# Turning gathered rows with a transposing DMA instead of TensorE, from the fourth tile of a mixture-of-experts layer on

## The reference, cut to what matters

```python
xt = x.reshape(b * l, d)
S = jax.nn.sigmoid(xt @ Wg)
G, I = jax.lax.top_k(S, TOP_K)
h = jax.nn.gelu(jnp.einsum('nd,edf->enf', xt, W1) + b1[:, None, :])
y = jnp.einsum('enf,efd->end', h, W2) + b2[:, None, :]
combine = jnp.zeros((N, E), dtype=x.dtype).at[jnp.arange(N)[:, None], I].add(G)
out = jnp.einsum('ne,end->nd', combine, y)
```

## Time and profile before

| | |
|---|---|
| median of three runs | 334.2 us (334.05 to 336.1) |
| the profiled execution | 335.84 us |
| its span, first to last instruction | 333.9 us |
| TensorE busy | 302.5 us (91%) |
| VectorE, ScalarE, GpSimd busy | 250.0, 179.7, 161.7 us |
| mean granted TensorE clock | 0.964 of full speed |
| DMA traffic | 39.41 MB, 118 GB/s over the span |

### The profile page before, as it was taken

How to read it: one execution, slowest core, us unless ns; L and a number is a source line. 1 busy time by engine, 2 the same in 40 slices (tenths; PEclk the granted TensorE clock), 3 DMA queues, 4 the chain that set the end, 5 groups by cost and what they waited for, 6 DMA issues and landing times.

```text
span 333.9 us, 8685 instructions
## 1 busy us (share of the span) xinstructions
PE 302.5 (91%) x3050; PEld 228.3 (68%) x3050; DVE 250.0 (75%) x596; ACT 179.7 (54%) x507; POOL 161.7 (48%) x162
## 2 busy tenths in 40 slices
PE   8999999999411898999999999999999999999991
PEld 8777534566311486888888888878777888877760
DVE  5898796779899799888888888887764656566441
ACT  4557484626815285676666667666534444434430
POOL 2415902556410732664456573365566647646353
PEclk9999999999955899999999999999999999999997
DMA  7400000011578294878667877764344544344421
GB/s 238 159 2 1 2 0 1 0 64 63 184 237 253 69 302 149 206 200 204 194 197 180 219 174 223 167 181 78 69 69 84 82 89 73 66 76 64 64 26 12
DMA packets 36361, 39.41 MB, mean 118 GB/s; under 512 B 8448, under 2 KB 32992, under 8 KB 36320
## 3 DMA queue, kind: packets, MB, share of 16 engines
q1 hardware_dynamic: 29344, 29.56, 30.1%
q0 software_dynamic: 6976, 9.31, 16.2%
HBM read 29.74 MB, written 9.11 MB: 116 GB/s over the span
## 4 chain that ended last, share of the span: by engine, by line
PE 58%; DMA 18%; DVE 13%; issue 6%; POOL 3%; POOLq 2%; ACT 0%
DMA out<-xt,idx 17%; PE ps L918 10%; PE ps L762 6%; PE ps L903 5%; PE ps L905 5%; PE ps L907 5%; PE ps L919 5%; PE ps L743 4%; PE ps L771 2%; PE ps L775 2%; PE ps L778 2%; PE ps L694 2%; PE ps L857 2%; PE ps L851 2%; PE ps L715 1%
## 5 line engine op out<-in xcount | busy, mean ns | idle before, releaser
L680 ACT ACTIVATE fb<-ps,b1t 128x128 f32<-128x128 f32 (+7 forms) x312 | 81.7, 374 | 83.5 <-issue 75.2
L918 PE MATMUL ps<-wt,fb 128*128 x312 | 117.0, 379 | 0.0
L903 PE MATMUL ps<-fb,wt 128*128 128x128 f16 (+7 forms) x624 | 114.3, 214 | 2.6 <-DVE fb L1368 2.6
L907 PE MATMUL ps<-fb,wt 128*128 128x128 f16 (+7 forms) x624 | 114.2, 214 | 0.0
L905 PE MATMUL ps<-fb,wt 128*128 128x128 f16 (+7 forms) x624 | 114.2, 214 | 0.0
L536 POOL DMA_INDIRECT out<-xt,idx x39 | 65.7, 1686 | 91.5 <-DMA out<-xt,idx 54.2
L919 PE MATMUL ps<-wt,fb 128*128 x312 | 85.0, 272 | 0.0
L903 PEld LDWEIGHTS ps<-fb,wt 128*128 x624 | 60.9, 98 | 32.9 <-issue 3.1
L524 POOL DMA_INDIRECT fb<-xn_rows,idx x39 | 53.6, 1373 | 24.4 <-DVE idx L1346 12.8
L905 PEld LDWEIGHTS ps<-fb,wt 128*128 x624 | 60.4, 98 | 3.3
L907 PEld LDWEIGHTS ps<-fb,wt 128*128 x624 | 60.4, 98 | 0.0
(11 more groups left out here) (208 smaller groups left out, 390.0 us busy)
## 6 DMA issues: line engine op xcount, KB each, us to landing
wt<-w SPq DMA_DIRECT2D x32, 512.0 KB, 4.2
b2t<-b SPq DMA_DIRECT2D x39, 128.0 KB, 3.5
out<-xt SPq DMA_DIRECT2D x8, 256.0 KB, 2.1
xn_rows<-wt SPq DMA_DIRECT2D x8, 256.0 KB, 3.2
xt<-x_tok SPq DMA_DIRECT2D x4, 256.0 KB, 4.2
xt<-x_tok SPq DMA_DIRECT2D x2, 512.0 KB, 7.1
b1t<-params SPq DMA_DIRECT2D x39, 4.0 KB, 2.7
fb<-xn_rows,idx POOLq DMA_INDIRECT x39
```

What stands on the lines that cost most here:

```text
L680: a = nc.scalar.activation(hid[:, s, f * P:f * P + ROWS[n]], h_ps(s)[:, f * P:f * P + ROWS[n]], ACT.Gelu_apprx_tanh, bias=b1t[:, n % NBIAS ...
L903: pe.matmul(dst, hi, xT[:, s, c * P:c * P + rows], start=(c == 0 and f % 4 == 0), stop=False, skip_group_check=True)
L907: m = pe.matmul(dst, lo, xT[:, s, c * P:c * P + rows], start=False, stop=(c == DC - 1), skip_group_check=True)
L918: pe.matmul(y_ps(s), hhi[:, s, f * P:(f + 1) * P], w, start=(f == 0), stop=False)
```

## The change

Tiles 0 to 2 (`PE_TURNED = 3`) go the old way. From tile 3 on the fetched rows are split first, as they lie (`rows_hi` on ScalarE, `rows_lo` on VectorE, into three slots `xsp`), and SP then issues one transposing DMA per tile (`turn_rows`) from `xsp` to `xT`, which now has four slots. Both lie in a part of `xt` that is free by then. The split of tile n+2 is in pass n, where the split of turned tile n+1 was. TensorE waits for the DMA (`xT_in`) instead of VectorE's subtract, and `gather(i)` waits for `rows_split` of the tile that had its slot, instead of TensorE's transposes.

```diff
+PE_TURNED = 3
+NSP, NXT = 3, 4
...
-        xT = view(1024, 512, F16).rearrange("p (s n) -> p s n", s=2)
+        xt_rest = xt[:, NYB:NBLK, :].rearrange("p k c -> p (k c)").bitcast(F16)
+        xT = xt_rest[:, 0:NXT * 2 * C].rearrange("p (s n) -> p s n", s=NXT)
+        xsp = xt_rest[:, NXT * 2 * C:(NXT + NSP) * 2 * C].rearrange("p (s n) -> p s n", s=NSP)
...
+            def turn_rows(n):
+
+                sp.wait_ge(rows_split, n - PE_TURNED + 1)
+                if n >= NXT:
+                    sp.wait_ge(l1_mm, n - NXT + 1)
+                sp.dma_start_transpose(xT[:, n % NXT, :].rearrange("p (j r) -> p j r", r=P)[:, :, 0:ROWS[n]],
+                                       xsp[0:ROWS[n], n % NSP, :]).then_inc(xT_in[n % NXT], 16)
+
+            turn_rows(PE_TURNED)
             for n in range(1, TILES):
                 for h in quarters_at(n):
                     if h + NSTG < NQ:
                         load(h + NSTG)
+                if n + PE_TURNED < TILES:
+                    turn_rows(n + PE_TURNED)
                 if NBIAS <= n + 2 < TILES:
                     biases(n + 2)
...
-                if i >= UNROLL:
+                if UNROLL <= i < UNROLL + PE_TURNED:
                     pool.wait_ge(xT_mm, i - (UNROLL - 1))
+                if i >= UNROLL + PE_TURNED:
+                    pool.wait_ge(rows_split, i - UNROLL - PE_TURNED + 1)
...
+            def rows_hi(n):
+
+                act.wait_ge(g_in[n % UNROLL], 16 * (n // UNROLL) + 16)
+                if n >= PE_TURNED + NSP:
+                    act.wait_ge(xT_in[(n - NSP) % NXT], 16 * turned_count(n - NSP))
+                nc.scalar.activation(xsp[0:ROWS[n], n % NSP, 0:C], xg[0:ROWS[n], n % UNROLL, :], ACT.Copy)\
+                    .then_inc(xThi_done, 1)
...
-                if n + 1 < TILES:
+                if n + 1 < PE_TURNED:
                     turned_hi(n + 1)
+                if PE_TURNED <= n + 2 < TILES:
+                    rows_hi(n + 2)
...
-                if one:
+                if one and n < PE_TURNED:
                     pe.wait_ge(xT_done, n + 1)
+                elif one:
+                    pe.wait_ge(xT_in[n % NXT], 16 * turned_count(n))
...
-                    if f == 1 and n + 1 < TILES:
+                    if f == 1 and n + 1 < PE_TURNED:
                         turn(n + 1)
...
+            def rows_lo(n):
+
+                dve.wait_ge(xThi_done, n + 1)
+                r = slice(0, ROWS[n])
+                v.tensor_tensor(out=xsp[r, n % NSP, C:2 * C], in0=xg[r, n % UNROLL, :], in1=xsp[r, n % NSP, 0:C],
+                                op=ALU.subtract).then_inc(rows_split, 1)
...
-                if 2 <= n < TILES - 1:
-                    rows_T(n + 1)
+                if PE_TURNED <= n + 2 < TILES:
+                    rows_lo(n + 2)
```

More of the change, by code:

```diff
@@ L318, in build @@
         xT_done = sem("xT_done")
+        rows_split = sem("rows_split")
+        xT_in = [sem(f"xT_in{i}") for i in range(NXT)]
         l1_mm = sem("l1_mm")
@@ L353, in cut, with turned_count @@
             return t.rearrange("p (f r) -> p f r", r=P)[:, :, 0:ROWS[n]]
+        def turned_count(n):
+            return len(range(PE_TURNED + (n - PE_TURNED) % NXT, n + 1, NXT))
         w1_dram = w1.rearrange("e (c p) f -> e p c f", p=P)
@@ L648, in turned_hi @@
                 act.wait_ge(xT_mm, n + 1)
-                if n >= 2:
-                    act.wait_ge(l1_mm, n - 1)
-                nc.scalar.activation(cut(xT[:, n % 2, 0:C], n), cut(xT_ps, n), ACT.Copy).then_inc(xThi_done, 1)
+                nc.scalar.activation(cut(xT[:, n % NXT, 0:C], n), cut(xT_ps, n), ACT.Copy).then_inc(xThi_done, 1)
+            def rows_hi(n):
[4 more added lines that the diff above has]
+                    .then_inc(xThi_done, 1)
             for u in range(B):
@@ L902, in first @@
                         lo = piece(e1, PIECE + c * F + f * P, P)
-                        pe.matmul(dst, hi, xT[:, s, c * P:c * P + rows], start=(c == 0 and f % 4 == 0), stop=False,
+                        pe.matmul(dst, hi, xT[:, n % NXT, c * P:c * P + rows], start=(c == 0 and f % 4 == 0), stop=False,
                                   skip_group_check=True)
-                        pe.matmul(dst, hi, xT[:, s, (2 + c) * P:(2 + c) * P + rows], start=False, stop=False,
+                        pe.matmul(dst, hi, xT[:, n % NXT, (2 + c) * P:(2 + c) * P + rows], start=False, stop=False,
                                   skip_group_check=True)
-                        m = pe.matmul(dst, lo, xT[:, s, c * P:c * P + rows], start=False, stop=(c == DC - 1),
+                        m = pe.matmul(dst, lo, xT[:, n % NXT, c * P:c * P + rows], start=False, stop=(c == DC - 1),
                                       skip_group_check=True)
@@ L1366, in rows_T @@
                 dve.wait_ge(xThi_done, n + 1)
-                at = xT[:, n % 2, :]
+                at = xT[:, n % NXT, :]
                 v.tensor_tensor(out=cut(at[:, C:2 * C], n), in0=cut(xT_ps, n), in1=cut(at[:, 0:C], n), op=ALU.subtract).then_inc(xT_done, 1)
+            def rows_lo(n):
[3 more added lines that the diff above has]
+                                op=ALU.subtract).then_inc(rows_split, 1)
             def gate_pay():
```

## The result

The changed kernel takes 351.25 us (median of 4 runs, 350.55 to 354.63) beside 334.34 us for the kernel before: a ratio of 1.0509, 95% interval 1.0460 to 1.0557, or 17 us slower. The forecast was 341.2 us: its sign was right, its size less than half (7.0 of 17 us); the range, 331 to 357 us, holds the result. Ratios are taken over undisturbed executions alone; where a kernel also had disturbed ones (e5, e8), its median over all runs lies a little higher than its ratio says. The profiled execution took 350.77 us with a span of 348.9, 15.0 us more than before.

What follows compares the result with a forecast made beforehand. The prediction took the chain of scatter-adds to bound the kernel, with TensorE running ahead. Its terms, -0.9 + 0.4 + 7.5 = +7.0 us on 334.2 us, gave 341.2 us, range 331 to 357 us.

Steps and rivals of the forecast that it cites:

- the biases behind the transposing DMA: On SP, biases of tile n+2 stand behind the waiting transposing DMA; wanted a step and a half later, so never late.
- The weights' half of the same sentence: On SP, the next weights behind the transposing DMA wait for a later VectorE instruction anyway, so they do not become late.
- What bounds the kernel: In the tile loop, the chain of scatter-adds sets the end from add 4 to the last, 176.45 us.
- -0.9 us: On TensorE, of 7.9 us of removed transposes only the turns of tiles 4 to 7 count: 4 x 0.22 us.
- TensorE runs ahead: From add 4 on, TensorE's tiles are ready before their adds: 12.6 us at tile 18, 3.0 us at tile 38.
- The load on the adds: On the DMA engines, 36 added DMAs slow the scatter-adds by 0.25 us over 30 intervals: +7.5 us.
- the late gather: On ScalarE, a late gather holds rows_hi(n+2) and the GELU behind it; tiles ahead of their adds pay: no cost.
- The +0.4 us at the start: On VectorE, one more subtract in step 1 delays what follows by 0.42 us and reaches step 3: +0.4 us.
- The wait of TensorE for the rows: TensorE waits for xT_in: 6.1 us remain, landings 3.1 to 3.8 us, 6.9 at worst; transposed rows mostly arrive in time.
- No contention: Rival: the added DMAs fit in the gaps of the adds, leaving only -0.5 us: 333.7 us; chance 0.21.
- Heavy transposes: Rival: each transposing DMA costs the adds 1.1 us and rows arrive late: 367 us; chance 0.15.
- Faster: Rival: earlier weights speed the chain of adds until the end follows TensorE: 326.7 us; chance 0.14.

Runs made afterwards that it cites:

- e5: Kernel before, without the two transposes per tile from tile 3 on (a one-column product instead; output not the reference's): 333.57 us, ratio 0.9944.
- e8: e1 with TensorE turning tiles 0 to 21 and the transposing DMA only tiles 22 to 38: 338.07 us, ratio 1.0064.
- e1: Changed kernel with the biases of tile n+2 issued ahead of the transposing DMA of tile n+3 on SP: 342.99 us, ratio 1.0271.
- e3: Kernel before, still turning on TensorE, plus an idle transposing DMA per tile from tile 4 on, issued behind the biases: 343.31 us, ratio 1.0242.
- e6: e3 with the idle transposing DMA and its wait placed ahead of the biases on SP: 354.08 us, ratio 1.0626.
- e10: Changed kernel with five bias slots, the biases of tile n+2 issued ahead of the transposing DMA on SP: 342.93 us, ratio 1.0232.
- e7: Changed kernel, its order on SP kept, with five bias slots and biases requested one tile earlier: 352.56 us, ratio 1.0515.
- e11: Kernel before without transposes from tile 3 on and without bias loads from tile 4 on (output not the reference's): 327.07 us, ratio 0.9815.
- e4: Kernel before with the two transposes of each tile from tile 3 on issued twice: 341.29 us, ratio 1.0201.
- e9: Kernel before without bias loads from tile 4 on (later tiles reuse the first tiles' biases; output not the reference's): 334.45 us, ratio 1.0001.
- e2: e1 with plain copies of the same bytes instead of transposing DMAs, rows not turned (output not the reference's): 339.31 us, ratio 1.0124.

## Why the prediction was right or wrong

**The step that failed: the biases behind the transposing DMA, costed at nothing.** I wrote that they "are wanted a step and a half later", so that "neither becomes late". Measured: putting them ahead again gives 8.3 us back (e1), and the reverse exchange in e3 costs 10.8 us (e6). With 8.3 us more in the sum the forecast would have been 349.5 us beside the 351.25 measured.

I had counted from the wrong instruction. A step and a half is the lead that the biases had before: they were issued 8.9 us (median) ahead of their GELU. The transposing DMA waits for the split of tile n+3, which VectorE makes late in the pass, behind `halves`; the biases of tile n+2 then pay SP's 1.21 us, two register loads and a landing of 3.8 us and more. From the end of that pass's subtract to the GELU there are 6.5 us in the kernel before (139.09 to 145.59 us, for instance). The changed kernel needs 6.7 us from the end of the split to the landing after the weights (236.84 to 243.58 us), and 7.3 us beside them (185.24 to 192.51 us). So the biases come too late for most GELUs. And the loss is not a fixed lateness: since the GELU leads over `halves` to the next split, it closes a ring, which the chain holds three times.

Beside the weights, where nearly all of the loss lies, it is shown that the order costs it (e1, e6, e10), but not by which path: e7 is without the GELU's waits and no faster there. The weights' half of the same sentence held: after 131 us ScalarE waited for no weight, before or after the change.

**What bounds the kernel: half right.** That the chain of adds keeps freed TensorE time from being worth much holds: -0.9 us forecast, -1.9 us measured alone (e5). But "TensorE runs ahead" was misread. The adds' 17% is the largest line of the chain only because TensorE's share is spread over many lines; by engine the page of the kernel before says:

```profile
PE 58%; DMA 18%; DVE 13%; issue 6%; POOL 3%; POOLq 2%; ACT 0%
```

And TensorE was busy for 91.37 of the 92.00 us from 140 to 232 us (the row above, at e11). One doubling of the transposes costs 6.7 us (e4), one relief of the adds gains nothing (e9), and both reliefs gain 6.2 us (e11). The lag of the last add, 3.0 us, was the number to go by: it bounds the slack between the two.

**The load on the adds: right in size, partly by luck.** Forecast 0.25 x 30 = 7.5 us; measured 8.6 us (e1) and 9.0 us (e3). Its composition was not as told. Plain copies leave 4.9 us (e2), and the turning adds 3.7, which I took as nothing. The landings were to be 0.2 to 0.4 us longer in both stages; under the load alone (e3) they are 0.9 us longer after the weights and no longer beside them. In e1 they are 4.6 and 5.4 us, in the changed kernel 4.2 and 6.7.

A second term at nothing was the late gather: "paid by tiles that run ahead of their adds", I wrote. In e1 ScalarE waited 50.5 us for gathers ahead of the GELU, and the result of tile 18 came 3.2 us later than before. No run takes this wait away by itself.

The Trainium skill, Advanced Engine Details and Errata, section X-Bar Transpose (TRN2), has transposing DMAs as fast as regular ones. Here the trace does not agree: 0.78 to 0.90 us of the engines against 0.44 to 0.46 us for the same bytes, and 3.7 us in the end (e1 against e2).

**The +0.4 us at the start.** From its step 2 to its step 3 TensorE took 8.22 us where it took 8.11, and result 2 came 0.1 us later than before; nothing larger is there to be seen, and it was not tried by itself.

**The wait of TensorE for the rows: nearly right.** 7 of 36 tiles waited, 9.4 us in all. Two early landings, in the chain of waits of the changed kernel, are above the 6.9 us that I took for the worst:

```profile
139.55 8.19 DMA xt<-xt
...
159.58 7.10 DMA xt<-xt
```

With adds that lag little there, such a tile costs its lateness: TensorE waited 2.7 us for the first of the two at the head of step 6, and the result of tile 4, made in that step, came at 156.2 us, 3.0 later than before.

**The rivals.** No contention is refuted by e3. Heavy transposes (367 us) fell as well: with the order mended 343 us remain, the engine time of one is twice a copy's and not four times, and in e1 its landing had medians of 3.3 us beside the weights and 4.3 us after them, not beyond 6. Faster fell too, though its sign appeared: adds late in the run waited for VectorE. They did because the results became later, not because the adds became quicker, so that sign alone tells nothing; it has to be read with the times of the results.

## What to carry to other kernels

When a DMA that waits is put into an engine's program, follow each instruction behind it from the moment the wait ends, not from where it stood before, and look whether its consumer leads back to that wait; a ring so closed can set the pace. Where two bounds lie within a few us, moving work from one to the other's resource loses what it costs and gains next to nothing: read the slack between them (here the lag of the last add, and how little TensorE stood idle) before pricing either side. Halving one suspect tells little there; take both away once, as in e11, to see what each was worth.

## What was not expected of the hardware

The transposing DMAs (128 x 512 two-byte numbers, fewer in the last tiles) went out as some 490 packets each in the mean, of about 240 bytes, and used twice the engine time of a copy. The issue of one also holds SP long, against 0.33 us for a plain load; the changed kernel's line L457 (min, median, max ns, first and last start):

```profile
L457 SPq DMA_TRANSPOSE xt<-xt x36: 1145/1203/1824, 126.1 to 328.8; - x36
```

And with the engines full, the rank of the small loads behind a transposing DMA (e7 against e10) decided 9.6 us, for a reason that these runs leave open.
